# Norms of finished panels by TensorE from the unturned sums, the turned sums scaled and added by VectorE out of PSUM

## The reference

```
layer 0:  A' = alpha*adj + (1-alpha)*I;  y = relu((A' @ x / rowsum(A')) @ W.T + b);  x1 = layernorm(x + y)
layer 1:  t  = x1 * artanh(|x1|) / |x1|                       # per row
          s  = sum over j of adj[i,j]*sig(l_i + r_j)*t_j  +  adj[j,i]*sig(l'_i + r'_j)*t_j
          n  = |s| per row;   v = tanh(n) * s / n;   v = v / |v| * 0.99999 where |v| is above 0.99999
          out = layernorm(x1 + v)
```

## Time and profile before

| | us |
|---|---|
| median of three runs | 2270.47 (2269.53 to 2271.97) |
| profiled execution | 2267.84 |
| its span | 2266.0 |
| VectorE busy over the span | 1983.8 (88%) |
| TensorE busy over the span | 1964.4 (87%) |
| GpSimd busy over the span | 1355.3 (60%) |
| ScalarE busy over the span | 1349.4 (60%) |
| last key of the last unit starts | 2238.38 |

### The profile page before, as it was taken

How to read it: one execution, slowest core, us unless ns; L and a number is a source line. 1 busy time by engine, 2 the same in 40 slices (tenths; PEclk the granted TensorE clock), 3 DMA queues, 4 the chain that set the end, 5 groups by cost and what they waited for, 6 DMA issues and landing times. The chain is left out here.

```text
span 2266.0 us, 17584 instructions
## 1 busy us (share of the span) xinstructions
PE 1964.4 (87%) x4652; PEld 829.8 (37%) x4652; DVE 1983.8 (88%) x1881; ACT 1349.4 (60%) x1640; POOL 1355.3 (60%) x559
## 2 busy tenths in 40 slices
PE   8999999999999989989999867887777778777774
PEld 3444444444444434434434323232222223222221
DVE  4676978988989988998999888999999999999995
ACT  0011324344364454453453687998889899898986
POOL 0000305436455455543444777999898998989995
PEclk9999999999999999999999988999999999999998
DMA  9998989899899988988888998999999999999993
GB/s 309 340 351 308 371 296 385 359 355 396 325 372 417 382 338 353 375 348 343 371 347 351 420 410 317 399 420 421 421 389 421 420 406 414 399 423 396 421 398 127
DMA packets 132083, 839.19 MB, mean 370 GB/s; under 512 B 15232, under 2 KB 27776, under 8 KB 33680
## 3 DMA queue, kind: packets, MB, share of 16 engines
q1 hardware_dynamic: 125184, 817.94, 90.5%
q10 hardware_dynamic: 6800, 20.13, 2.3%
HBM read 829.56 MB, written 8.45 MB: 370 GB/s over the span
## 5 line engine op out<-in xcount | busy, mean ns | idle before, releaser
L494 POOL TENSOR_TENSOR chi<-chi,ring 128x1024 f32<-128x1024 f32 x320 | 819.0, 2569 | 662.5 <-ACT chi L646 598.8
L1125 PE MATMUL ps<-keys,xtA 128*128 128x512 f32 x1720 | 847.1, 620 | 189.0 <-DVE keys L925 170.5
L1056 PE MATMUL ps<-ring,xA 128*128 128x512 f32 x2048 | 921.5, 600 | 37.1 <-DMA ring<-in_g_blk 32.9
L660 ACT ACTIVATE ps<-scores,prcr 128x1024 f32<-128x1024 f32 x512 | 567.8, 1109 | 435.9 <-DVE keys L925 417.4
L823 DVE TENSOR_TENSOR dsum<-dsum,ring 128x2048 f32<-128x2048 f32 x240 | 592.8, 2470 | 43.5 <-DMA ring<-in_g_blk 36.3
L914 DVE TENSOR_TENSOR ps<-ps,ring 128x1024 f32<-128x1024 f32 x440 | 537.7, 1222 | 66.6 <-ACT ps L660 62.7
L925 DVE TENSOR_TENSOR keys<-ps,chi 128x1024 f32<-128x1024 f32 x430 | 526.5, 1224 | 72.2 <-issue 39.4
L1056 PEld LDWEIGHTS ps<-ring,xA 128*128 128x128 f32 x2048 | 387.0, 192 | 531.3 <-issue 469.5
L1125 PEld LDWEIGHTS ps<-keys,xtA 128*128 128x128 f32 x1720 | 316.6, 195 | 688.2 <-issue 664.1
L646 ACT ACTIVATE chi<-scores,prcr 128x1024 f32<-128x1024 f32 x430 | 488.4, 1136 | 14.5 <-DMA scores<-plcl_d 6.7
L494 POOL TENSOR_TENSOR chi<-chi,xA 128x1024 f32<-128x1024 f32 x110 | 259.0, 2367 | 41.5 <-ACT chi L646 39.6
(11 more groups left out here) (99 smaller groups left out, 645.7 us busy)
## 6 DMA issues: line engine op xcount, KB each, us to landing
ring<-in_g_blk SPq DMA_DIRECT2D x476, 1024.0 KB, 9.8
ring<-in_a_cols SPq DMA_DIRECT2D x185, 1024.0 KB, 9.0
xA<-in_a_cols SPq DMA_DIRECT2D x71, 1024.0 KB, 9.5
xA<-in_g_blk SPq DMA_DIRECT2D x36, 1024.0 KB, 10.8
scores<-plcl_d ACTq DMA_DIRECT2D x22, 512.0 KB, 11.2
xA<-in_x_g SPq DMA_DIRECT2D x64, 64.0 KB, 13.2
yb<-in_xT ACTq DMA_DIRECT2D x8, 512.0 KB, 8.9
x_d<-res ACTq DMA_DIRECT2D x8, 512.0 KB, 9.0
```

Source lines behind the costliest of these rows:

```text
L494: pool.tensor_tensor(out=chi(n), in0=chi(n), in1=half(t, n), op=ALU.mult).then_inc(m2_ready, 1)
L660: act.activation(slots[s], scores[:, row, 0, :], ACT.Sigmoid, bias=prcr[:, 2 * jt:2 * jt + 1]).then_inc(p_ready, 1)
L1056: ins = pe.matmul(Y[:, h * BANK:(h + 1) * BANK], xA[:, tile * D:(tile + 1) * D], t[:, tt * BP + h * BANK:tt * BP + (h + 1) * BANK], start= ...
L1125: ins = pe.matmul(outp[:, h * BANK:(h + 1) * BANK], xtA[:, jt * D:(jt + 1) * D], keys(n)[:, h * BANK:(h + 1) * BANK], start=begins, stop=i ...
```

## The change

The order of the work on a finished panel becomes:

- the sum is taken out of `outp` as before (+3)
- ScalarE squares the unturned sum whole, 128x1024, into the other half of `dsum` (`sqT`, +4)
- TensorE sums the squares over the partitions by eight fp32 products of 128 columns with a column of ones (`norms`, +4), into a slot that is taken before unit +6 and set free by the root
- ScalarE takes the root out of PSUM (+7), with the previous panel's deviation; VectorE's floor is at +8, inverse at +9 with the previous panel's inverse, its shift at +10, the other factor steps at +11 to +16; tanh at +12; ScalarE normalises the previous panel at +13 to +20
- TensorE turns the sum at +14 into a slot taken before unit +16; VectorE scales it out of PSUM and adds the residual in eight parts at +17, in place in the residual's buffer; statistics at +18 to +25, aggregates at +26
- GpSimd has no part in it any more. The copy to uN is gone. SP stores the previous panel at +36

```diff
-F_EVAC, F_TURN, F_SLOT, F_COPY, F_SQUARE, F_ROOT, F_FLOOR, F_INV, F_RSTD, F_TANH, F_CHAIN, F_NORM, F_SCALE, F_ADD, \
-    F_STATS, F_AGGR = 3, 2, 4, 5, 6, 15, 17, 18, 18, 19, 21, 20, 29, 31, 33, 42
+F_EVAC, F_SQUARE, F_NORMS, F_NORMS_SLOT, F_ROOT, F_FLOOR, F_INV, F_RSTD, F_TANH, F_CHAIN, F_NORM, F_TURN, F_SLOT, \
+    F_ADD, F_STATS, F_AGGR = 3, 4, 4, 6, 7, 8, 9, 9, 12, 11, 13, 14, 16, 17, 18, 26
-F_STORE = 42
-L_ROOT, L_RSTD, L_NORM = 47, 49, 52
+F_STORE = 36
+L_ROOT, L_RSTD, L_NORM = 34, 36, 38
...
         if n in starts:
-            uses.append(("final", starts[n], n))
+            uses.append(starts[n] + (n,))
         uses.append(("unit", n, n))
-    uses.append(("final", len(FINALS) - 1, UNITS))
+    uses += [("norms", len(FINALS) - 1, UNITS), ("final", len(FINALS) - 1, UNITS)]
...
+        def slot_free(eng, before):
+            kind, i = before
+            if kind == "unit":
+                eng.wait_ge(k_ready, i + 1)
+            elif kind == "norms":
+                eng.wait_ge(f_norm, i + 1)
+            elif kind == "final":
+                eng.wait_ge(v_ready, i + 1)
...
-            def scale(k):
-                pool.wait_ge(f_step, f_steps(k, F_STEPS))
-                pool.wait_ge(sq_ready, k + 1)
-                pool.tensor_tensor(out=u3, in0=u3, in1=s_s[:, at].unsqueeze(2).to_broadcast([P, TPP, D]),
-                                   op=ALU.mult).then_inc(scaled, 1)
-            def add_residual(k):
-                pool.wait_ge(scaled, k + 1)
-                pool.wait_ge(x1f_in[k % 2], 16 * (k // 2 + 1))
-                pool.tensor_tensor(out=x1f[k % 2][:, :], in0=uN, in1=x1f[k % 2][:, :], op=ALU.add).then_inc(v_ready, 1)
...
-            def copy_turned(k):
-                act.activation(uN, slots[SLOT_OF_FINAL[k][0]], ACT.Copy).then_inc(uN_ready, 1)
-            def square(k, i):
-                ins = act.activation(uT[:, i * D:(i + 1) * D], uN[:, i * D:(i + 1) * D], ACT.Square,
-                                     accum_out=s_ss[:, k * TPP + i:k * TPP + i + 1])
+            def square(k):
+                p, _ = FINALS[k]
+                act.wait_ge(out_evac, GROUP_OF_FINAL[k] + 1)
+                act.wait_ge(norms_ready, k)
+                act.activation(sqT, uT if p >= EARLY else acc[:, p * BP:(p + 1) * BP], ACT.Square).then_inc(sq_ready, 1)
             def norm(k):
-                act.wait_ge(sq_ready, k + 1)
-                act.activation(s_n[:, at], s_ss[:, at], ACT.Sqrt).then_inc(f_norm, 1)
+                act.wait_ge(norms_ready, k + 1)
+                act.activation(s_n[:, at], slots[SLOT_OF_NORMS[k][0]][:, 0:TPP], ACT.Sqrt).then_inc(f_norm, 1)
...
+            def add_residual(k):
+                dve.wait_ge(f_step, f_steps(k, F_STEPS))
+                dve.wait_ge(uT_ready, k + 1)
+                dve.wait_ge(x1f_in[k % 2], 16 * (k // 2 + 1))
+                for i in range(TPP):
+                    t, j = x1f[k % 2][:, i * D:(i + 1) * D], k * TPP + i
+                    ins = dve.scalar_tensor_tensor(out=t, in0=slots[SLOT_OF_FINAL[k][0]][:, i * D:(i + 1) * D],
+                                                   scalar=s_s[:, j:j + 1], in1=t, op0=ALU.mult, op1=ALU.add)
+                ins.then_inc(v_ready, 1)
...
+            def norms(k):
+                pe.wait_ge(sq_ready, k + 1)
+                s, before = SLOT_OF_NORMS[k]
+                slot_free(pe, before)
+                for j in range(TPP):
+                    ins = pe.matmul(slots[s][:, j:j + 1], columns(sqT, j), ones[:, 0:1], start=True, stop=True)
+                ins.then_inc(norms_ready, 1)
```

More of the change, by code:

```diff
@@ L135, in slot_plan @@
 def slot_plan():
-    of_unit, of_final, holder, turn = {}, {}, {0: ("layer 0", 0), 1: ("passage", 0), 2: None}, 0
-    starts = {b + F_SLOT: k for k, (_, b) in enumerate(FINALS)}
+    plans = {"unit": {}, "norms": {}, "final": {}}
+    holder = {0: ("layer 0", 0), 1: ("passage", 0), 2: None}
+    starts = {b + F_NORMS_SLOT: ("norms", k) for k, (_, b) in enumerate(FINALS)}
+    starts |= {b + F_SLOT: ("final", k) for k, (_, b) in enumerate(FINALS)}
     uses = []
@@ L153, in slot_plan @@
         last = s
-        (of_unit if kind == "unit" else of_final)[i] = (s, holder[s])
+        plans[kind][i] = (s, holder[s])
         holder[s] = (kind, i)
-    return of_unit, of_final
-SLOT_OF_UNIT, SLOT_OF_FINAL = slot_plan()
+    return plans["unit"], plans["norms"], plans["final"]
+SLOT_OF_UNIT, SLOT_OF_NORMS, SLOT_OF_FINAL = slot_plan()
 def load_plan():
@@ L300, in adj_resnorm_kernel @@
          dg, sf, rc, inv, mb) = [small[:, k, :] for k in range(21)]
-        fs = sb("fs", [P, 11, UPP])
+        fs = sb("fs", [P, 10, UPP])
         mvf = sb("mvf", [P, UPP, 2])
         bstf = sb("bstf", [P, TPP, 6])
-        s_n, s_nm, s_th, s_rn, s_s1, s_n2, s_s, s_sd, s_rs, s_mb, s_ss = [fs[:, k, :] for k in range(11)]
+        s_n, s_nm, s_th, s_rn, s_s1, s_n2, s_s, s_sd, s_rs, s_mb = [fs[:, k, :] for k in range(10)]
         uT = dsum[:, 0:BP]
-        uN = dsum[:, BP:2 * BP]
+        sqT = dsum[:, BP:2 * BP]
         x1f = [yb, res]
@@ L390, in adj_resnorm_kernel @@
         uT_ready = sem("uT_ready")
-        uN_ready = sem("uN_ready")
+        norms_ready = sem("norms_ready")
         sq_ready = sem("sq_ready")
@@ L396, in adj_resnorm_kernel @@
         f_dev = sem("f_dev")
-        scaled = sem("scaled")
         x1f_in = [sem(f"x1f_in{k}") for k in range(2)]
@@ L407, in adj_resnorm_kernel @@
         N_CONST = 9
+        def slot_free(eng, before):
[6 more added lines that the diff above has]
+                eng.wait_ge(v_ready, i + 1)
+            elif kind == "layer 0":
+                eng.wait_ge(y_evac, NPAN)
+            else:
+                eng.wait_ge(rows_ready, NPAN)
+                eng.wait_ge(prcr_ready, NPAN)
         block = ctx.enter_context(nc.Block())
@@ L503, in add_taken @@
                 pool.tensor_tensor(out=at, in0=taken[:, :], in1=at, op=ALU.add).then_inc(acc_added, 1)
-            def scale(k):
-                at = slice(k * TPP, (k + 1) * TPP)
-                u3 = uN.rearrange("p (t d) -> p t d", t=TPP)
-                pool.wait_ge(f_step, f_steps(k, F_STEPS))
-                pool.wait_ge(sq_ready, k + 1)
-                pool.tensor_tensor(out=u3, in0=u3, in1=s_s[:, at].unsqueeze(2).to_broadcast([P, TPP, D]),
-                                   op=ALU.mult).then_inc(scaled, 1)
-            def add_residual(k):
-                pool.wait_ge(scaled, k + 1)
-                pool.wait_ge(x1f_in[k % 2], 16 * (k // 2 + 1))
-                pool.tensor_tensor(out=x1f[k % 2][:, :], in0=uN, in1=x1f[k % 2][:, :], op=ALU.add).then_inc(v_ready, 1)
             for g in range(PAIRS):
@@ L528, in _ @@
                     fold(NPAN - 1)
[L529 to L533, removed]
                 second_product(n)
@@ L536, in _ @@
                     add_taken(EVAC_AT_UNIT[n])
-            scale(NPAN - 1)
-            add_residual(NPAN - 1)
         @block.scalar
@@ L649, in sigmoids @@
                 if before is not None:
[L650 to L659, removed]
+                    slot_free(act, before)
                 act.activation(slots[s], scores[:, row, 0, :], ACT.Sigmoid,
@@ L682, in evacuate @@
                 act.wait_ge(uT_ready, k)
-                act.wait_ge(sq_ready, k)
                 act.activation(uT, outp, ACT.Copy).then_inc(out_evac, 1)
@@ L689, in evacuate_early_panel @@
                 act.activation(acc[:, p * BP:(p + 1) * BP], outp, ACT.Copy).then_inc(out_evac, 1)
-            def copy_turned(k):
-                act.wait_ge(uT_ready, k + 1)
-                act.wait_ge(v_ready, k)
-                act.activation(uN, slots[SLOT_OF_FINAL[k][0]], ACT.Copy).then_inc(uN_ready, 1)
-            def square(k, i):
-                if i == 0:
-                    act.wait_ge(uN_ready, k + 1)
-                ins = act.activation(uT[:, i * D:(i + 1) * D], uN[:, i * D:(i + 1) * D], ACT.Square,
-                                     accum_out=s_ss[:, k * TPP + i:k * TPP + i + 1])
-                if i == TPP - 1:
-                    ins.then_inc(sq_ready, 1)
+            def square(k):
[3 more added lines that the diff above has]
+                act.activation(sqT, uT if p >= EARLY else acc[:, p * BP:(p + 1) * BP], ACT.Square).then_inc(sq_ready, 1)
             def norm(k):
                 at = slice(k * TPP, (k + 1) * TPP)
-                act.wait_ge(sq_ready, k + 1)
-                act.activation(s_n[:, at], s_ss[:, at], ACT.Sqrt).then_inc(f_norm, 1)
+                act.wait_ge(norms_ready, k + 1)
+                act.activation(s_n[:, at], slots[SLOT_OF_NORMS[k][0]][:, 0:TPP], ACT.Sqrt).then_inc(f_norm, 1)
             def final_deviation(k):
@@ L730, in final @@
                     evacuate(k)
[L731 to L734, removed]
+                if step == F_SQUARE:
+                    square(k)
                 if step == F_ROOT:
@@ L787, in _ @@
             evacuate(k)
-            copy_turned(k)
-            for i in range(TPP):
```

(11 more changed lines are left out.)

## The result

| | before | after |
|---|---|---|
| median, runs timed together | 2270.0 us (2266.4 to 2271.97, 4 runs) | 2293.19 us (2292.5 to 2294.24, 4 runs) |
| ratio, 95% interval | | 1.0102 (1.0084 to 1.012) |
| profiled execution, its span | 2267.84, 2266.0 | 2293.48, 2291.7 |
| key of unit 232 starts | 1496.16 | 1498.02 |
| last key starts | 2238.38 | 2269.08 |

The change makes the kernel 1% slower, 23 us by the medians.

The account below looks back on a forecast made before the run. VectorE was taken as the bound. Panels cost 13.4 us for six and 12.6 for the first, 93, less 72.6: +20.5; tail -5.1; +15.4 on 2270.47, said as 2285, range 2256 to 2297.

Parts of the forecast that it names:

- What bounds the kernel: Units 232 to 511: VectorE sets the pace at 2.40 us a unit; seven finished panels cost 72.6 us beyond that.
- Items 1 and 2: GpSimd's scale and add go, -2.8 us for each of six panels; VectorE gets eight PSUM multiply-adds, +2.07 us a panel.
- Item 5: Norms' PSUM slot before unit +6 shortens ScalarE's lead; VectorE waits 1.9 us a panel around +7, bounds 0.4 and 4.3.
- The small steps: VectorE's small steps at +8 to +16 wait for GpSimd's multiplies: 6.6 us a panel, bounds 1.0 and 16.
- Item 6: Shift at +10 ends ScalarE's wait for it, -0.5 us; that wait had let GpSimd run dry, keeping small steps in gaps.
- Blind chance: Seven exposed small steps meeting GpSimd's multiplies at random: 7.5 us a panel, total about 2293.
- Tail: Last panel, evacuation to statistics: statistics start 5.1 us earlier, bounds -3.8 (table loads behind the sums) and -5.4.
- Lock-step: Rival: after the shift, small steps fall into GpSimd's gaps, waits 3.0 us a panel, 2262; chance 0.23 together with cancelling.
- Late norms: Rival: norms' chain on TensorE later, root waits and VectorE 2 us more a panel, 14 in all: 2299; chance 0.09.
- The loads: Rival: DMA becomes the bound, only with over 30 us won; chance 0.01.

Follow-up runs that it names:

- run without a table change: Changed kernel with the roots of the seven in-loop panels' norms and six variances replaced by copies, so ScalarE changes no activation table there: 2277.37 us.
- run with one empty unit: Changed kernel with the six factor steps behind tanh, turn, multiply-adds and statistics one unit later, leaving +11 without a small step: 2265.31 us.
- run with reciprocals: Changed kernel with each small VectorE step that GpSimd can hold replaced by a reciprocal of same size, place and waits; factor not computed: 2245.76 us.
- kernel with all steps on GpSimd: Changed kernel with six of eight factor steps (all but reciprocals) and the previous panel's shift moved to GpSimd for the in-loop panels: 2245.02 us.

## Why the prediction was right

The forecast was slower, 2285 (2256 to 2297); 2293.19 was measured. The range held a gain as well, and a time above 2275 was given a chance of 0.64. By its own steps:

- **What bounds the kernel.** Right. VectorE sets the pace. ScalarE and GpSimd lost work and nothing came of it.
- **Items 1 and 2.** Right in size: eight multiply-adds last 2.15 us in a panel and lengthen its unit to 4.46, 2.06 over 2.40; the 2.20 us wait of +31 is gone. In the first panel there was nothing to save, as written.
- **Item 5, the lead of ScalarE.** Forecast 1.6 and 0.25 us; measured 1.61 and 0.25, where before had 0.38 and 0.26. The run without a table change prices it at 2.3 with what it does to the floor.
- **The small steps.** The working by turns of GpSimd gave holds of 1.0, 1.9, 2.2, 0.5 and "2.1 or nothing" for floor, shift, L919, L921, L923. Measured, as unit times of the sixth panel beyond 2.48: 0.94, 1.92, 2.15, 0.42, 2.15, together 7.6. So the term mis-sized is the last: I took 6.6 us a panel as a mean over a near tie of 0.09 us, which went the same way in all six panels. With 7.6 the excess is 6 x 14.4 + 13.8 (the first panel, by its unit times, where 12.6 was forecast) = 100, against 101.5 measured and 93 forecast. That is 7 of the 8 us missing in the total. (The sum itself, 2270.47 + 15.4, gives 2285.9, not 2285.5.)
- **Item 6.** Its first half is right, the shift at +10 is held and so was the one in the old kernel once ScalarE did not wait. Its second half is right as a way but not the only one: in the changed kernel ScalarE's wait alone, without an empty unit, brings the old pattern back (shift 0.16 us, first product 1.29, then 0.16 to 0.23; before had 0.16, 1.25, 0.16). But the old kernel did not depend on the wait, since without it the later steps stayed free: the empty unit behind the shift is enough too. The prediction did not see the empty unit.
- **Blind chance.** The rule of the Trainium skill (SBUF - State Buffer, section Who interferes with whom) names those who are held, and every held step here has two SBUF inputs or is a tensor_scalar, while reciprocals and the multiply-adds out of PSUM are free. Priced by chance it came near (7.5 against 7.6 us a panel, and its total of about 2293 is the one measured), but that is luck: the run with one empty unit has the same exposed steps and only some 3.2 us of holds (0.94, 1.93, 0.18 and 0.10 beyond 2.48 in its units +8, +10, +13 and +16 of the sixth panel).
- **Tail.** -5.1 forecast, -5.0 measured; the table loads during the sums, as taken.
- **Rivals.** Lock-step did not come in this kernel; it is what the kernels with an empty unit or a waiting ScalarE show, at 2265 to 2266 where 2262 had been worked out. Late norms did not come: ScalarE never waited for them inside the loop. (The time that TensorE has free, 30% in that rival, is 24% by the earlier trace rows: 566.14 of 740 us are busy.) The loads did not bind this kernel; VectorE waits for one only in the run with reciprocals.

## What to carry to other kernels

Where VectorE and GpSimd both stream, a 0.16 us VectorE instruction with two SBUF inputs, or a tensor_scalar, can cost as much as the GpSimd instruction it meets, and the profile books it as busy time: compare the mean duration of small instructions with their minimum before moving them. Spread such steps by where they meet GpSimd, not evenly: with two engines of nearly the same period, here 2.40 and 2.32 us, steps in the units right behind a held one were held again (L919 and L923 whole, L921 0.42 us), and a gap of one unit ended it in the six panels with a shift. It is no general cure: in the first panel two units without such a step stand ahead of the first product (+9 has only a reciprocal, +10 nothing), and it is held. The best kernel here had them on GpSimd itself; a form that is not held would do as well, as the reciprocals show; an operand in PSUM frees the multiply-adds, and was not tried for small steps.

## What was not expected of the hardware

- Near ties of 0.05 to 0.08 us between GpSimd's start and VectorE's request were decided the same way in all six panels with a shift (L919 and L923), so they can be worked out rather than averaged.
- ScalarE's wait for VectorE made the kernel faster (2266.32 against 2293.19).
- The sums against a column of ones took 2.05 us in the tail of the kernel after and 3.57 us in that of the kernel with all steps on GpSimd. In the windows of 6 us around them the granted clock of TensorE is 0.81 and 0.62 of 2.4 GHz, means over a time at 2.4 and one at 1.2; in both kernels it had been 1.00 in the window of 5 us before, and TensorE stood still for 2.20 us just ahead of the sums. This is the 1.5 us of the longer tail; why it fell earlier in one than in the other stays open.

```profile
2273.00:2279.00 6.00, 3.81 (x24) 3.41 (x24) 0.81 (x5) 5.07 (x7) 0.00 (x0) 0.81 0.00 0
```

```profile
2223.00:2229.00 6.00, 4.50 (x21) 4.50 (x22) 0.38 (x2) 3.57 (x5) 0.00 (x0) 0.62 0.00 0
```

(busy us and records of TensorE, its weight loads, VectorE, ScalarE and GpSimd, then the clock, DMA share and GB/s; the kernel after first)
